# Routing logits as further columns of both products of stage one

## The chip, the cores and the metric

The kernel runs on one core of a Trainium2 chip. The metric is device time in microseconds for one execution; the median of three runs stands beside one profiled execution, whose trace is read below.

## The reference

```python
# x: (4, 512, 512) float32, ctx: (4 experts, 512, 512), 8 experts in the second layer
h = layernorm(x)                                  # (x - mean) / sqrt(var + 1e-5)
e1 = token_ids // 6250                            # expert of the first layer, by token id
a = h @ ctx[e1].T
x = x + (silu(a) * a) @ ctx[e1].T                 # the same ctx is gate, up and down matrix
h = layernorm(x)
idx = argmax(h @ router_w.T)                      # expert of the second layer, 8 logits
xq = act_quant(h)                                 # int8 steps by row
g, u = xq @ ternary(wg[idx]).T, xq @ ternary(wu[idx]).T
x = x + act_quant(relu(g) ** 2 * u) @ ternary(wd[idx]).T
```

`ternary(w)` rounds w / mean(|w|) to -1, 0 or 1 and scales back. There are 24 such matrices of 512 x 512.

## The kernel before

The 2048 rows are sorted by their first expert into B1 = 19 blocks of 128 rows (some padded), which stage one computes; stage two sorts them again by the chosen expert into B2 = 23 slots. Every engine has a queue that is written out by hand and runs in order; semaphores join them.

**Stage one** is a loop over ticks t. Both products of a block (`product1`, L1576) keep float32 accuracy with a high and a low half of each operand: hi x hi, hi x lo and lo x hi, each over K = 4 chunks of 128, so 12 matmuls of 512 columns in float32r. In tick t TensorE runs, in this order: transposes of p of block t-1 (L1560), first product of block t, `rank` of block t-3, transposes of the new row x1 of block t-2 (L1560, `transpose_x1`), transposes of h of block t+1, `sum_mean` (L1595), second product of block t-1, `logits` of block t-2 (L1668: x1 transposed, times router, 8 columns, float32, two instructions each), `count_in` of block t-3.

ScalarE in tick t: `evict_pT` (L739), `square` (L747), `silu` (L758), `evict_x1T` (L767, the copy of the transposed row that `logits` reads), `evict_hT` (L775), `scale_part` (L711, 1536 of the 2048 columns of a row of weight matrix t+2), in some ticks `scale_piece` (L731), `sum_abs` (L705) of weight matrix t+3, in some ticks `sum_piece` (L720).

VectorE in tick t: `residual` (L1121) of block t-2, `top_logits`, `choice` and `one_hot` of block t-3, `normalise`, `pT_rest` (L1110, the low half of p transposed), `largest`, `gate` (L1101), `mean_of` and `scale_of` (L1015, L1021) of matrix t+2, which release ScalarE's `scale_part`, its own `scale_part` (L1026, 512 columns), `row_index`, `hT_rest`, `moments_of`, and `cut` (L1032).

Two of the 24 weight matrices (21 and 22, `EXTRA`) don't fit the row of one a tick. Their sums are made in four pieces each, in ticks 3 to 6 and 11 to 14, and their scaling in three, in ticks 8 to 10 and 16 to 18.

SP issues the loads in order (`load_weights`, L382): matrix i waits until ScalarE and VectorE have scaled the matrix that had its buffer. The first extra matrix (L404) goes out behind weights 6, the second (L407) behind weights 14; behind weights 12 goes a 2 MB filler. After the last tick SP loads the rows of stage two (L411); loads 0 to 2 wait for matrix 20 to be scaled, loads 3 and 4 for matrix 21, by both engines:

```python
for s in range(EARLY):
    if s % 3 == 0:
        sp.wait_ge(dve_part, len(ORDER) - 1 + s // 3)
        sp.wait_ge(act_part, len(ORDER) - 1 + s // 3)
    load(s)
```

GpSimd gathers the rows of a block (L482), makes the scales of a row, and scatters it (L571) to the place of its expert.

Of the kernel before, what the change touches and what calls it, by code (L numbers as in the profile page):

```python
# [61 lines left out]

RING, ROWS = 5, 3
# [30 lines left out]
def moe_program(nc, x_in, tokens_in, ctx_in, router_in, weights_in, out):  # L94
    with ExitStack() as whole:
# [10 lines left out]
        bank = [whole.enter_context(nc.psum_tensor(f"bank{i}", [P, D], F32)) for i in range(8)]  # L106
# [10 lines left out]
        x1T = sb("x1T", [P, D], F32)  # L117
# [49 lines left out]
        best = sb("best", [P, 8], F32)  # L167
        best_at = sb("best_at", [P, 8], U32)
# [48 lines left out]
        with ExitStack() as inner:  # L217
            stack.append(inner)
            h = sb("h", [P, D], F32)
            hT_lo = sb("hT_lo", [P, D], F32R)  # L220
            ctx_hi = sb("ctx_hi", [P, E1 * K * D], F32R)
            ctx_lo = sb("ctx_lo", [P, E1 * K * D], F32R)
            stack.pop()
# [16 lines left out]
        assert ORDER[-1] % 3 == 2  # L240

# [28 lines left out]
        a_ps = [bank[4], bank[5]]  # L270
# [55 lines left out]
        x1T_ready, x1T_copied, logits_ready = (sem(n) for n in ("x1T_ready", "x1T_copied", "logits_ready"))  # L326
        best_ready, choice_ready, onehot_ready = sem("best_ready"), sem("choice_ready"), sem("onehot_ready")
# [39 lines left out]
        def _(sp):  # L367
# [5 lines left out]
            def load_weights(i):  # L373
# [58 lines left out]
        def _(pool):  # L432
# [53 lines left out]
            def high_halves(e):  # L486
# [3 lines left out]
                pool.tensor_copy(ctx_hi[:, e * K * D:(e + 1) * K * D], ctx_raw[e]).then_inc(pool_hi_ready, 1)  # L490
# [99 lines left out]
            for t in range(TICKS):  # L590
                if t >= 2:
                    gather(t + 3)
                if t < B1:
                    quantising(t - 2)
                    place(t - 3)
                    store(t - 3)
# [62 lines left out]
            place(B1 - 3)  # L659
            scale_of(B1 - 2)  # L660
            ratio_of(B1 - 2)
            store(B1 - 3)
            deviation_of(B1 - 1)
            place(B1 - 2)
            roots_of(B1 - 1)
            store(B1 - 2)
            scale_of(B1 - 1)
            place(B1 - 1)
# [15 lines left out]
        def _(act):  # L684
            act.preload_act_table(ACT.Silu)
            def high_halves(e):
                act.wait_ge(ctx_in_sem[e], 16)
                nc.scalar.activation(ctx_hi[:, e * K * D:(e + 1) * K * D], ctx_raw[e], ACT.Copy)\
                    .then_inc(ctx_hi_ready, 1)

            def sum_abs(i):
# [3 lines left out]
                if m == X_MATRIX:  # L695

                    act.wait_ge(x1_ready, X_USERS[-1] + 1)
                if m > EXTRA[1]:
# [25 lines left out]
            def scale_piece(x, j):  # L724
                m, first, end = EXTRA[x], EXTRA_CUTS[j], EXTRA_CUTS[j + 1]
                act.wait_ge(extra_scale_ready, x + 1)
                if j == 0:
# [23 lines left out]
            def silu(b):  # L751
# [4 lines left out]
                if b >= 1:  # L756
                    act.wait_ge(pT_ready, b)
                nc.scalar.activation(p[:, :], a_ps[b % 2][:, :], ACT.Silu, scale=rstd1[b % 2][:, :])\  # L758
                    .then_inc(sil_ready, 1)

            def evict_x1T(b):
                if not 0 <= b < B1:
# [4 lines left out]
                nc.scalar.activation(x1T[:, :], x1T_ps[:, :], ACT.Copy).then_inc(x1T_copied, 1)  # L767
# [86 lines left out]
            for t in range(2, TICKS):  # L854
# [4 lines left out]
                silu(t)  # L859
                evict_x1T(t - 2)  # L860
                evict_hT(t + 1)
                if t == 2:
# [12 lines left out]
            evict_x1T(B1 - 1)  # L875
# [30 lines left out]
        def _(dve):  # L906
# [94 lines left out]
            def low_half(e, part):  # L1001

                first = part * K * D // 2
                cols = slice(e * K * D + first, e * K * D + first + K * D // 2)
                if part == 0:
                    dve.wait_ge(*((ctx_hi_ready, e + 1) if e < 2 else (pool_hi_ready, e - 1)))
                ins = dve.tensor_tensor(ctx_lo[:, cols], ctx_raw[e][:, first:first + K * D // 2],  # L1007
                                        ctx_hi[:, cols].bitcast(F32), ALU.subtract)
                if part == 1:
                    ins.then_inc(ctx_lo_ready, 1)  # L1010

# [11 lines left out]
            def scale_part(i):  # L1023
                m = ORDER[i]
# [10 lines left out]
            def cut(i):  # L1035
                dve.wait_ge(dve_part, i + 1)
# [60 lines left out]
            def gate(b):  # L1097
# [3 lines left out]
                dve.scalar_tensor_tensor(p[:, :], a_ps[b % 2][:, :], rstd1[b % 2][:, :], p[:, :],  # L1101
# [11 lines left out]
            def residual(b):  # L1113
# [7 lines left out]
                dve.scalar_tensor_tensor(row[b % ROWS][:, 0:D], y_ps[:, :], 1.0, x[b % RING], ALU.mult,  # L1121
# [16 lines left out]

            def top_logits(b):
                if not 0 <= b < B1:  # L1140
                    return
                dve.wait_ge(logits_ready, b + 1)
                dve.max(best[:, :], logits_ps[:, 0:E2]).then_inc(best_ready, 1)

            def choice(b):
# [3 lines left out]
                dve.max_index(best_at[:, :], best[:, :], logits_ps[:, 0:E2]).then_inc(choice_ready, 1)  # L1149
# [258 lines left out]
            for t in range(2, TICKS):  # L1408
                interlude = early if t == EARLY_AFTER + 4 else iter(())
                residual(t - 2)  # L1410
                top_logits(t - 3)
                negative_mean(t - 2)
                next(interlude, None)
                choice(t - 3)
                next(interlude, None)
                one_hot(t - 3)
                next(interlude, None)
                normalise(t + 1)
                if t == 3:
# [3 lines left out]
                pT_rest(t - 1)  # L1423
                if t == 2:
# [6 lines left out]
                if t == 2:  # L1431
                    scale_part(3)
                next(interlude, None)
                gate(t)
# [489 lines left out]
```

## Time and profile before

| | us |
|---|---|
| median of 3 runs (lowest, highest) | 252.63 (252.18, 252.65) |
| the profiled execution | 252.44 |
| its span, first to last instruction | 250.5 |
| stage one, silu 0 to silu 18 | 21.66 to 162.75 |
| granted TensorE clock, mean | 0.993 |

"Busy" is the time in which an engine has an instruction running. Matmuls are pipelined, so the distance from one group's start to the next is what a group costs; its own duration is longer. "Idle before" is the engine's idle time ahead of an instruction, with what ended it.

### The profile page before, as it was taken

How to read it: one execution, taken by the hardware profiler on the slowest of the kernel's cores; microseconds unless marked ns; L12 is line 12 of the kernel's file. 1: busy time of each engine (PE TensorE's matmuls, PEld its weight loads, DVE VectorE, ACT ScalarE, POOL GpSimd, SP SyncE). 2: the span in 40 equal slices, each digit the busy share in tenths (PEclk: the TensorE clock that was granted, in tenths of full speed). 3: DMA queues.
4: the chain of work that ended last, by engine and by line, in shares of the span. 5: the costliest groups of instructions: out<-in, count | busy, mean ns of one | idle time of the engine just before them, and what ended most of it. 6: DMA issues, size and time to landing. Idle time of an engine off the chain costs nothing.

```text
span 250.5 us, 5540 instructions
## 1 busy us (share of the span) xinstructions
PE 230.1 (92%) x1319; PEld 168.0 (67%) x1327; DVE 216.7 (87%) x675; ACT 208.7 (83%) x324; POOL 166.1 (66%) x325
## 2 busy tenths in 40 slices
PE   2398999999999999999999999999989999999980
PEld 2245788888888888888888888887335445454430
DVE  5979999989898888898889888969999999999881
ACT  2767799799889888898889878888889999999970
POOL 4362675868778777778777745345737788686863
PEclk9999999999999999999999999999999999999997
DMA  5999953946753589885764545534358982212110
GB/s 194 425 357 361 429 210 107 377 154 238 252 184 102 193 306 404 285 311 207 252 218 139 176 185 213 174 98 152 99 149 258 303 294 93 99 69 79 66 42 0
DMA packets 13725, 51.70 MB, mean 206 GB/s; under 512 B 2750, under 2 KB 2750, under 8 KB 10112
## 3 DMA queue, kind: packets, MB, share of 16 engines
q1 hardware_dynamic: 8816, 37.91, 43.0%
q0 software_dynamic: 4880, 13.44, 14.6%
q8 instruction: 13, 0.21, 0.3%
q14 instruction: 16, 0.13, 0.1%
HBM read 40.49 MB, written 13.48 MB: 215 GB/s over the span
## 4 chain that ended last, share of the span: by engine, by line
PE 76%; DVE 11%; DMA 5%; ACT 3%; issue 3%; POOL 0%; SPq 0%; DVEq 0%; ACTq 0%
PE bank L1576 35%; PE bank L1698 22%; PE bank L1560 9%; PE bank L1668 5%; DMA ternary<-weight_chunks 3%; PE bank L1690 2%; PE bank L1802 2%; DVE ctx_lo L1007 1%; DMA staged<-x_rows 1%; PE bank L1595 1%; DVE ternary L964 1%; ACT ternary L705 1%; DVE p L1101 1%; DMA token_ids<-token_ids_in 1%; DVE ternary L1026 1%
## 5 line engine op out<-in xcount | busy, mean ns | idle before, releaser
L1698 PE MATMUL bank<-ternary,qT 128*128 x178 | 45.1, 379 | 0.5
L705 ACT ACTIVATE ternary<-staged 128x2048 bf16<-128x2048 f32 x20 | 38.0, 1900 | 2.0 <-DMA staged<-weight_chunks 2.0
L711 ACT ACTIVATE ternary<-staged,w_scale 128x1536 int16<-128x1536 f32 x20 | 31.4, 1576 | 2.3 <-DVE w_scale L1021 0.6
L571 POOL DMA_INDIRECT x_rows<-row,store_at x19 | 25.5, 1343 | 6.8 <-POOL store_at L563 5.0
L1698 PEld LDWEIGHTS bank<-ternary,qT 128*128 128x128 bf16 x184 | 17.2, 98 | 16.3 <-issue 1.0
L482 POOL DMA_INDIRECT x<-x_rows,gather x16 | 18.5, 1155 | 10.3 <-DVE gather L976 6.5
L652 POOL DMA_INDIRECT out_rows<-late_rows,late_token x18 | 19.6, 1089 | 7.9 <-DVE late_rows L1366 5.5
L1698 PE MATMUL bank<-ternary,rT 128*128 x90 | 23.4, 379 | 1.4 <-ACT rT L809 0.8
L758 ACT ACTIVATE p<-bank,rstd 128x512 f32<-128x512 f32 x19 | 13.0, 686 | 12.6 <-PE bank L1576 12.6
L1101 DVE SCALAR_TENSOR_TENSOR p<-bank,rstd,p 128x512 f32<-128x512 f32 x19 | 14.2, 749 | 9.6 <-ACT p L758 9.6
L1576 PE MATMUL bank<-ctx_hi,pT_hi 128*128 x76 | 22.3, 415 | 0.1
L1576 PE MATMUL bank<-ctx_hi,hT_hi 128*128 x76 | 22.4, 416 | 0.0
L1668 PEld LDWEIGHTS bank<-router,x1T 128*128 128x128 f32 x152 | 19.7, 191 | 2.0 <-ACT x1T L767 0.6
L1576 PE MATMUL bank<-ctx_lo,hT_hi 128*128 x76 | 20.4, 390 | 0.2 <-DVE ctx_lo L1007 0.2
L1576 PE MATMUL bank<-ctx_lo,pT_hi 128*128 x76 | 20.5, 392 | 0.0
L1576 PE MATMUL bank<-ctx_hi,pT_lo 128*128 x76 | 20.5, 392 | 0.0
L526 POOL TENSOR_TENSOR row<-ln,half_powers 128x2 f32<-128x2 f32 x19 | 14.5, 763 | 8.8 <-DVE squares L1136 8.7
L1576 PE MATMUL bank<-ctx_hi,hT_lo 128*128 x76 | 20.3, 389 | 0.0
L1668 PE MATMUL bank<-router,x1T 128*128 128x8 f32 x152 | 18.2, 246 | 0.1
L1312 DVE TENSOR_TENSOR prod<-bank,relu 128x512 f32<-128x512 f32 x23 | 15.9, 690 | 2.1 <-issue 0.8
L498 POOL TENSOR_TENSOR rstd<-var_eps,half_powers 128x1 f32<-128x1 f32 x19 | 13.7, 719 | 5.3 <-DVE var_eps L1077 4.8
L1576 PEld LDWEIGHTS bank<-ctx_lo,hT_hi 128*128 128x128 f32 x76 | 14.2, 188 | 3.6 <-issue 0.6
(237 smaller groups left out, 650.9 us busy)
## 6 DMA issues: line engine op xcount, KB each, us to landing
staged<-weight_chunks SPq DMA_DIRECT2D x20, 1024.0 KB, 5.4
late_rows<-x_rows SPq DMA_DIRECT2D x18, 260.0 KB, 3.7
ternary<-ctx_chunks SPq DMA_DIRECT2D x4, 1024.0 KB, 8.3
ternary<-weight_chunks SPq DMA_DIRECT2D x4, 1024.0 KB, 9.4
x_rows<-filler SPq DMA_DIRECT2D x1, 2080.0 KB, 12.6
staged<-x_rows SPq DMA_DIRECT2D x5, 260.0 KB, 2.9
x_rows<-row,store_at POOLq DMA_INDIRECT x19, 6.2
out_rows<-late_rows,late_token POOLq DMA_INDIRECT x18, 2.8
```

Of the source, the lines that this page charges most:

```text
L482: pool.indirect_dma_start(x[b % RING], None, x_in, bass.IndirectOffsetOnAxis(ap=gather1[:, b:b + 1], axis=0), bounds_check=last_token, oob ...
L526: pool.tensor_tensor(r[:, RSTD:INV + 1], s[:, 2:4], half_powers[:, :], ALU.pow).then_inc(norm2, 1)
L571: pool.indirect_dma_start(x1_rows, bass.IndirectOffsetOnAxis(ap=store_at[b % ROWS][:, :], axis=0), row[b % ROWS][:, :], None, bounds_check ...
L652: pool.indirect_dma_start(out, bass.IndirectOffsetOnAxis(ap=token, axis=0), cols_of([b], 0, D), None, bounds_check=last_token, oob_is_err= ...
L705: nc.scalar.activation(ternary[:, m * K * D:(m + 1) * K * D], staged_of(i), ACT.Abs, accum_out=abs_sum[:, 2 * i:2 * i + 1]).then_inc(abs_r ...
L711: nc.scalar.activation(ternary[:, m * K * D + DVE_COLS:(m + 1) * K * D].bitcast(I16), staged_of(i)[:, DVE_COLS:], ACT.Copy, scale=w_scale[ ...
L1101: dve.scalar_tensor_tensor(p[:, :], a_ps[b % 2][:, :], rstd1[b % 2][:, :], p[:, :], ALU.mult, ALU.mult).then_inc(p_ready, 1)
L1312: dve.tensor_tensor(prod[b % 2][:, :], u_ps[b % 2][:, :], relu2[:, :], ALU.mult)\
L1560: last = pe.transpose(ps[:, k * P:(k + 1) * P], src[:, k * P:(k + 1) * P], ident[:, :])
L1576: last = pe.matmul(ps[:, :], left[:, k * P:(k + 1) * P], right[:, bass.ds(e * (K * D) + k * D, D)], start=(n == 0 and k == 0), stop=(n == ...
L1668: last = pe.matmul(logits_ps[:, 0:E2], x1T[:, k * P:(k + 1) * P], router[:, k * E2:(k + 1) * E2], start=(k == 0), stop=(k == K - 1))
L1698: last = pe.matmul(ps[:, :], side(left[:, :], k), ternary[:, bass.ds(e * (3 * K * D) + (kind * K + k) * D, D)], start=(k == 0), stop=(k == ...
```

## The change

The logits of a block are (x + y) times router, where y is the second product. Since y = p x ctx^T, the part y x router is p times (ctx^T x router), and the part x x router is likewise 8 columns beside the first product (h instead of x: the same order of logits). So each context gets 8 further columns on either side: on the left the router, for the first product, on the right "contexts times router", for the second. From block FOLD = 5 on the logits are the sum of the two, and the x1 transposes, their copy and `logits` are left out.

- 520 columns don't fit one bank, so each matmul becomes two, of 256 and 264 columns, in halves of two neighbouring banks (`columns_of`). The first product has one buffer instead of two.
- Contexts times router is made once, in ticks 4 and 5 (`cr_products`: 32 matmuls for two experts, float32, 32 columns of stationary on each of four column groups), from four more transfers of 1 MB (the contexts by rows, `load_rows`), copied by ScalarE (`copy_cr`), transposed (`cr_transposes`) and split into halves by VectorE (`cr_halves`). GpSimd pads the router (`pad_router`).
- VectorE keeps the 8 logits of the first product (`keep_logits`, between gate and mean) and adds those of the second (`sum_logits`, ahead of the residual). The choice comes one tick earlier.
- From matrix SOLO = 9 on ScalarE scales all 2048 columns and VectorE none; SP's loads wait for ScalarE alone from there.
- The early slot tables are made in tick 17 instead of 18.

```diff
+FOLD = 5
+LEFT, RIGHT = E2, E2 + D
+WIDTH = D + 2 * E2
+CR_TICK = FOLD - 1
+SOLO = FOLD + 2 + 2
...
-                    sp.wait_ge(dve_part, last + 1)
+                    sp.wait_ge(dve_part, min(last + 1, SOLO))
                     sp.wait_ge(act_part, last + 1)
...
+            def load_rows(e):
+                sp.wait_ge(ctx_lo_ready, (0, 0, 1, E1 - 1)[e]) if e > 1 else None
+                sp.dma_start(ctx_rows[e], ctx_rows_in[e]).then_inc(ctx_rows_in_sem[e], 16)
+
             for i in range(4, len(ORDER)):
                 load_weights(i)
+                if i == 5:
+                    load_rows(0)
+                    load_rows(1)
+                if i == 6:
+                    load_rows(2)
+                    load_rows(3)
...
                 if s % 3 == 0:
-                    sp.wait_ge(dve_part, len(ORDER) - 1 + s // 3)
                     sp.wait_ge(act_part, len(ORDER) - 1 + s // 3)
...
             def scale_part(i):
-                m = ORDER[i]
+                m, first = ORDER[i], DVE_COLS if i < SOLO else 0
                 act.wait_ge(w_scale_ready, i + 1)
-                nc.scalar.activation(ternary[:, m * K * D + DVE_COLS:(m + 1) * K * D].bitcast(I16),
-                                     staged_of(i)[:, DVE_COLS:], ACT.Copy, scale=w_scale[:, m:m + 1])\
+                nc.scalar.activation(ternary[:, m * K * D + first:(m + 1) * K * D].bitcast(I16),
+                                     staged_of(i)[:, first:], ACT.Copy, scale=w_scale[:, m:m + 1])\
                     .then_inc(act_part, 1)
...
+            def keep_logits(b):
+
+                if not FOLD <= b < B1:
+                    return
+                dve.wait_ge(sil_ready, b + 1)
...
+                dve.tensor_copy(own_logits[b % 2][:, :], own_ps).then_inc(kept_ready, 1)
+
+            def sum_logits(b):
...
+                dve.wait_ge(y_ready, b + 1)
+                dve.wait_ge(kept_ready, b - FOLD + 1)
...
+                dve.tensor_tensor(summed[:, :], carried_ps, own_logits[b % 2][:, :], ALU.add).then_inc(summed_ready, 1)
...
-                interlude = early if t == EARLY_AFTER + 4 else iter(())
+                interlude = early if t == EARLY_AFTER + 3 else iter(())
...
                     for k in range(K):
-                        last = pe.matmul(ps[:, :], left[:, k * P:(k + 1) * P],
-                                         right[:, bass.ds(e * (K * D) + k * D, D)],
-                                         start=(n == 0 and k == 0), stop=(n == 2 and k == K - 1))
+                        for ps, first, columns in pieces:
+                            last = pe.matmul(ps, left[:, k * P:(k + 1) * P],
+                                             right[:, bass.ds(e * (K * WIDTH) + k * WIDTH + first, columns)],
+                                             start=(n == 0 and k == 0), stop=(n == 2 and k == K - 1))
...
+            def columns_of(b, second):
+
+                half = D // 2
+                if b < FOLD:
+                    return [(y_ps[:, :] if second else bank[4 + b % 2][:, :], LEFT, D)]
+                if second:
+                    return [(bank[2][:, half:], LEFT, half), (bank[3][:, 0:half + E2], LEFT + half, half + E2)]
+                return [(bank[4][:, half - E2:], 0, half + E2), (bank[5][:, 0:half], LEFT + half, half)]
+
+            def cr_products(pair):
...
+                for i in range(2):
+                    pe.wait_ge(ctx_rows_in_sem[2 * pair + i], 16)
+                    for k in range(K):
+                        for g in range(K):
+                            last = pe.matmul(cr_ps[g * 32:(g + 1) * 32, i * P:(i + 1) * P],
+                                             router_pad[:, k * 32:(k + 1) * 32],
+                                             ctx_rows[2 * pair + i][:, k * D + g * P:k * D + (g + 1) * P],
+                                             start=(k == 0), stop=(k == K - 1))
+                last.then_inc(cr_ready, 1)
...
             def transpose_x1(b):
-                if not 0 <= b < B1:
+                if not 0 <= b < FOLD:
                     return
...
             def logits(b):
-                if not 0 <= b < B1:
+                if not 0 <= b < FOLD:
                     return
...
+                if t == CR_TICK:
+                    cr_products(0)
+                if t in (CR_TICK + 1, CR_TICK + 2):
+                    cr_transposes(t - CR_TICK - 1)
...
                 sum_mean(t + ABOVE)
+                if t == CR_TICK + 1:
+                    cr_products(1)
                 second_product(t - 1)
...
             transpose_q(0)
             load_ffn_expert(0)
-            transpose_x1(B1 - 1)
             sum_mean(B1 + ABOVE)
+            rank(B1 - 1)
             gate_product(0)
-            logits(B1 - 1)
-            rank(B1 - 2)
```

## Rows read from the trace of the kernel before

**Rows 1.** The page's first part: busy time of each engine.
```profile
PE 230.1 (92%) x1319; PEld 168.0 (67%) x1327; DVE 216.7 (87%) x675; ACT 208.7 (83%) x324; POOL 166.1 (66%) x325
```

**Rows 2.** Windows, silu to silu: length, busy us (instructions) by engine, PEclk, DMA.
```profile
67.00:74.98 7.98, 7.98 (x50) 6.80 (x50) 7.30 (x25) 6.93 (x11) 6.03 (x11) 1.00 0.59 197
...
154.77:162.75 7.98, 7.98 (x50) 6.80 (x50) 6.83 (x31) 7.07 (x10) 3.24 (x7) 1.00 0.49 166
```

**Rows 3.** Timeline of TensorE over one tick: start us, duration us, what.
```profile
99.81 1.17 PE L1576 MATMUL bank<-ctx_hi,pT_hi 128*128 x4
...
102.64 0.95 PE L1668 MATMUL bank<-router,x1T 128*128 128x8 f32 x8
103.45 0.17 PE L1685 MATMUL bank<-onehot,from 128*128 128x8 bf16 x1
103.48 0.64 PE L1560 MATMUL bank<-ident,p 128*128 128x128 f32 x4
103.87 1.17 PE L1576 MATMUL bank<-ctx_hi,hT_hi 128*128 x4
104.88 1.07 PE L1576 MATMUL bank<-ctx_lo,hT_hi 128*128 x4
...
106.73 0.63 PE L1560 MATMUL bank<-ident,row 128*128 128x128 f32 x4
107.20 0.60 PE L1560 MATMUL bank<-ident,h 128*128 128x128 f32 x4
107.78 1.17 PE L1576 MATMUL bank<-ctx_hi,pT_hi 128*128 x4
```

**Rows 4.** Timeline of ScalarE, ticks with and without a piece.
```profile
74.98 0.69 ACT L758 ACTIVATE p<-bank,rstd 128x512 f32<-128x512 f32 x1 [0.95 <-PE bank L1576]
...
83.53 0.59 ACT L767 ACTIVATE x1T<-bank 128x512 f32<-128x512 f32 x1
...
84.72 1.58 ACT L711 ACTIVATE ternary<-staged,w_scale 128x1536 int16<-128x1536 f32 x1
86.20 0.87 ACT L731 ACTIVATE ternary<-ternary,w_scale 128x704 int16<-128x704 f32 x1
...
90.94 0.69 ACT L758 ACTIVATE p<-bank,rstd 128x512 f32<-128x512 f32 x1 [0.79 <-PE bank L1576]
...
146.80 0.69 ACT L758 ACTIVATE p<-bank,rstd 128x512 f32<-128x512 f32 x1 [1.44 <-PE bank L1576]
```

**Rows 5.** Timeline of all engines in one tick: from silu to the scaling.
```profile
106.90 0.68 ACT L758 ACTIVATE p<-bank,rstd 128x512 f32<-128x512 f32 x1
...
107.64 0.75 DVE L1101 SCALAR_TENSOR_TENSOR p<-bank,rstd,p 128x512 f32<-128x512 f32 x1
...
108.31 0.15 DVE L1015 TENSOR_SCALAR w_mean<-bank 128x1 f32<-128x1 f32 x1
...
108.69 0.49 DVE L1026 TENSOR_SCALAR ternary<-staged,w_scale 128x512 int16<-128x512 f32 x1
```

**Rows 6.** Timeline in tick 3: the extra matrix's issue, its first piece, the product behind.
```profile
43.04 0.33 SPq L404 DMA_DIRECT2D ternary<-weight_chunks  x1
...
49.91 0.63 ACT L720 ACTIVATE dump<-ternary 128x512 bf16<-128x512 f32 x1 [1.20 <-DMA ternary<-weight_chunks]
...
51.90 1.20 PE L1576 MATMUL bank<-ctx_hi,pT_hi 128*128 x4
```

**Rows 7.** A window of tick 3 (last two: DMA share, GB/s), and ScalarE in tick 10.
```profile
43.00:45.00 2.00, 2.00 (x14) 1.73 (x13) 2.00 (x6) 2.00 (x5) 0.87 (x3) 1.00 0.98 412
...
103.81 1.91 ACT L705 ACTIVATE ternary<-staged 128x2048 bf16<-128x2048 f32 x1 [0.79 <-DMA staged<-weight_chunks]
```

**Rows 8.** Timeline at the end of stage one: last scaling, and loads 3 and 4.
```profile
173.64 1.57 ACT L711 ACTIVATE ternary<-staged,w_scale 128x1536 int16<-128x1536 f32 x1
...
175.16 0.48 DVE L1026 TENSOR_SCALAR ternary<-staged,w_scale 128x512 int16<-128x512 f32 x1
...
176.77 1.46 SPq L411 DMA_DIRECT2D staged<-x_rows  x2
```

More of the change, by code:

```diff
@@ L104, in moe_program @@
         x1_rows = nc.dram_tensor("x1_rows", [SCRATCH_ROWS, ROW], F32).ap()
-        bank = [whole.enter_context(nc.psum_tensor(f"bank{i}", [P, D], F32)) for i in range(8)]
+        banks = whole.enter_context(nc.psum_tensor("banks", [P, 8 * D], F32))
+        bank = [banks[:, i * D:(i + 1) * D] for i in range(8)]
         ternary = sb("ternary", [P, MATS * K * D], BF16)
@@ L167, in moe_program @@
         best = sb("best", [P, 8], F32)
+        own_logits = [sb(f"own_logits{i}", [P, E2], F32) for i in range(2)]
+        summed = sb("summed", [P, E2], F32)
         best_at = sb("best_at", [P, 8], U32)
@@ L240, in moe_program, with whole_chunks, beside @@
         assert ORDER[-1] % 3 == 2
+        ctx_rows = [spare(m, 2 * K * D, F32) for m in (12, 14, 16, 20)]
+        early_home = spare(18, 2 * K * D // 2, F32)
+        x1T, router_pad = early_home[:, 0:D], early_home[:, D:D + P]
+        crT = early_home[:, D + P:D + 3 * P]
+        def whole_chunks(halves, e):
+            return halves[:, :].rearrange("p (e k w) -> p e k w", e=E1, k=K)[:, e, :, LEFT:RIGHT]
+        def beside(halves, first):
+            return halves[:, :].rearrange("p (e k w) -> p e k w", e=E1, k=K)[:, :, :, first:first + E2]
         staged_early = [spare(8, 2 * K * D, F32), spare(10, 2 * K * D, F32)]
@@ L592, in _ @@
                     gather(t + 3)
+                if t == 3:
+                    pad_router()
+                if t == FOLD + 3:
+                    place(FOLD)
+                    store(FOLD)
                 if t < B1:
                     quantising(t - 2)
-                    place(t - 3)
-                    store(t - 3)
+                    place(chosen(t)[0])
+                    store(chosen(t)[0])
                 if t >= 2:
@@ L726, in scale_piece @@
                 act.wait_ge(extra_scale_ready, x + 1)
+                if x == 0 and j == 0:
+                    act.wait_ge(crT_ready, E1 // 2)
                 if j == 0:
@@ L766, in evict_x1T, with copy_cr @@
                     act.wait_ge(logits_ready, b)
-                nc.scalar.activation(x1T[:, :], x1T_ps[:, :], ACT.Copy).then_inc(x1T_copied, 1)
+                else:
+                    act.wait_ge(ctx_lo_ready, 2)
+                nc.scalar.activation(x1T, x1T_ps[:, :], ACT.Copy).then_inc(x1T_copied, 1)
+            def copy_cr(pair):
+                act.wait_ge(cr_ready, pair + 1)
+                if pair >= 1:
+                    act.wait_ge(crT_ready, pair)
+                nc.scalar.activation(crT, cr_ps, ACT.Copy).then_inc(cr_copied, 1)
             def evict_hT(b):
@@ new lines, in cr_halves @@
+            def cr_halves(pair):
+                two = slice(2 * pair, 2 * pair + 2)
+                made_of = cr_ps.rearrange("p (e k w) -> p e k w", e=2, k=K)[:, :, :, 0:E2]
+                high, low = (beside(halves, RIGHT)[:, two] for halves in (ctx_hi, ctx_lo))
+                dve.wait_ge(crT_ready, pair + 1)
+                dve.tensor_copy(high, made_of).then_inc(cr_halves_ready, 1)
+                dve.wait_ge(cr_halves_ready, 2 * pair + 1)
+                dve.tensor_tensor(low, made_of, high.bitcast(F32), ALU.subtract).then_inc(cr_halves_ready, 1)
@@ L1137, in largest, with logits_of @@
                                   accum_out=ln2[b % 2][:, 3:4]).then_inc(largest_ready, 1)
+            def logits_of(b):
+                return logits_ps[:, 0:E2] if b < FOLD else summed[:, :]
             def top_logits(b):
@@ L1408, in _ @@
             for t in range(2, TICKS):
-                interlude = early if t == EARLY_AFTER + 4 else iter(())
+                interlude = early if t == EARLY_AFTER + 3 else iter(())
+                first, *second = chosen(t)
+                sum_logits(t - 2)
                 residual(t - 2)
-                top_logits(t - 3)
+                if t == FOLD + 3:
+                    row_index(FOLD)
+                top_logits(first)
                 negative_mean(t - 2)
                 next(interlude, None)
-                choice(t - 3)
+                choice(first)
                 next(interlude, None)
-                one_hot(t - 3)
+                one_hot(first)
                 next(interlude, None)
+                for b in second:
+                    top_logits(b)
                 normalise(t + 1)
+                for b in second:
+                    choice(b)
+                    one_hot(b)
                 if t == 3:
@@ L1444, in _ @@
                 if t < B1:
-                    row_index(t - 3)
+                    row_index(first)
                 next(interlude, None)
@@ L1561, in transpose1, with product1 @@
                 return last
-            def product1(ps, hi, lo, e, b=None, ahead=None):
+            def product1(pieces, hi, lo, e, b=None, ahead=None):
                 pairs = [(hi, ctx_hi), (hi, ctx_lo), (lo, ctx_hi)]
@@ L1661, in logits @@
             def logits(b):
-                if not 0 <= b < B1:
+                if not 0 <= b < FOLD:
                     return
```

172 lines of the change are left out of this document (120 added, 52 removed).

## The prediction

> **What bounds the kernel now.** I read the page first: TensorE is busy for 92% of the span and its next rival, VectorE, for 87% [rows 1]. An average over two stages says little, so I cut stage one at each silu with the windows view. From silu 7 (74.98 us) to silu 18 (162.75) are eleven ticks of 7.98 us, and TensorE is busy for all of such a tick, while VectorE and ScalarE are busy for about 7 [rows 2, 4]. The reader is to see that TensorE sets the tick, and that what comes next is only one microsecond below. The timeline of TensorE then splits a tick, from one second product to the next (99.81 to 107.78, 7.97 us): second product 2.83; logits 0.81; transposes of p 0.39; first product with the rank behind it 2.86; transposes of the new row 0.47; transposes of h 0.44; the rest is a mean and a count [rows 3]. The change takes 0.81 + 0.47 = 1.28 us out of it, if nothing else comes to bind.
>
> What else can bind is read from ScalarE's queue, which is strictly in order: silu, x1T copy, hT copy, scaling of a weight matrix, a piece of an extra matrix in some ticks, absolute sum of the next matrix, pT copy, square, and the next silu. Its idle time before the next silu is its whole slack: 0.79 us in a tick with a scaling piece, 0.95 with a summing piece, 1.44 with none [rows 4]. What starts the scaling is not the x1T copy in front of it but VectorE: gate 0.74 us after the silu, mean and reciprocal after it; the scaling starts 1.79 us after the silu [rows 4, 5].
>
> **The change part by part.**
>
> 1. *Products in halves.* Each 512-column matmul becomes one of 256 and one of 264 columns, each with its own weight load: 24 pairs in place of 12. No row shows a 4-byte matmul of 256 columns with its load. Twelve of 512 take 2.83 us; its first four take 0.10 more than the next four (1.17 against 1.07 [rows 3]), so one costs 0.228 beside 0.09 once, of which 512 columns at 2.4 GHz are 0.213. Take 256 columns (0.107) away: 0.121, and 0.125 for 264; a product is 12 x 0.246 + 0.09 = 3.04, or 0.21 more. From below, the loads bound it: eight loads with 8-column matmuls come every 0.10 to 0.11, four transposes of 128 columns too [rows 3], so 24 x 0.11 = 2.6, a gain of 0.2. From above, load and stream not overlapped, 0.11 + 0.11 each: 5.3. The 512-column stream overlaps its loads and so do the transposes, so I take 3.04. TensorE's tick: 7.97 - 1.28 + 0.42 = 7.11 us.
>
> 2. *ScalarE.* The x1T copy (0.59) goes, but the scaling waits for VectorE anyway, so its place becomes idle time and gives nothing. From matrix 9 (tick 7) ScalarE scales all 2048 columns. From 704 to 1536 columns it grows by 0.71 us [rows 4], 0.85 ns a column, so 512 more cost 0.44. Keeping the 8 logits on VectorE stands between gate and mean and so ahead of the scaling: about 0.10, between nothing and the 0.15 that the small instruction there takes [rows 5]. ScalarE's cycle grows by 0.54: 7.98 - 0.79 + 0.54 = 7.73 in a tick with a scaling piece, 7.98 - 0.95 + 0.54 = 7.57 with a summing piece, 7.98 - 1.44 + 0.54 = 7.08 with none. That is above TensorE's 7.11 in all ticks but those without a piece: ScalarE becomes the bound and takes back more than half of the gain.
>
> 3. *VectorE.* It loses 0.4 (its part of the scaling [rows 5]) and gains two instructions of 8 columns: 7.30 in tick 6 to 7 [rows 2] becomes about 7.2. It hides behind the others except in tick 7 (7.2). In tick 17 it now makes the early slot tables as well, formerly a tick later: 31 instructions against 25 [rows 2] show the kind of load; I charge 0.3 there.
>
> 4. *Ticks 7 to 17.* 7.2 + 3 x 7.73 + 4 x 7.57 + 7.11 + 7.73 + 8.0 = 83.5 us, against 11 x 7.98 = 87.8: a gain of 4.3. (Scaling pieces are in ticks 8 to 10 and 16 to 18, summing pieces in 3 to 6 and 11 to 14.)
>
> 5. *Ticks 5 and 6* still do old work for blocks 3 and 4, and have four split products, 4 x 0.21, and four transposes of contexts times router, 4 x 0.11: +1.3.
>
> 6. *Contexts times router.* Per pair of experts 32 float32 matmuls of 128 columns, each two instructions; a 4-byte transpose of 128 columns takes 0.11 [rows 3], so 64 x 0.11 = 7.0 us if nothing overlaps, 1.8 if the four column groups run together. No row shows column groups. 64 loads and 64 matmuls must also be issued, so I take 3.5. The second pair stands in tick 5 ahead of the second product, with TensorE full: +3.5 (1.8 to 7.0). The Trainium skill, "TensorE: Matmul & The Clock Gate", section Part 3, measured 2.38 times for three column tiles. By that the pair would take 2.9 and the sum would be 0.6 lower, an estimate; no row here shows it. The first pair stands in tick 4 and is hidden, as follows.
>
> 7. *The new transfers.* Four matrices of 1 MB. The first two go out behind weights 5, when the engines are full, but nothing waits for what is behind them. The other two are issued on SP behind weights 6, ahead of the first extra matrix, which goes out at 43.04. ScalarE already waits 1.20 us for that matrix in tick 3 and starts its piece at 49.91; pT copy, square, silu are queued behind, VectorE's pT_lo behind those, and TensorE's second product starts at 51.90 because of it [rows 6]. At 412 GB/s, with the engines 98% busy in that stretch [rows 7], 2.1 MB more are 5.1 us. So ScalarE, then VectorE, then TensorE stand 5.1 us later: +5.1. The first pair of step 6 runs in this hole, as it stands on TensorE before the blocked product; at 7.0 it would stick out by 1.9.
>
> 8. *A later collision.* In tick 10 ScalarE waits 0.79 us for weights held up by the 2 MB of filler and an extra matrix [rows 7]; before, its slack took that. Now it has none, and the tick before is a quarter of a microsecond shorter: +1.1 (0 to 1.5).
>
> 9. *End of stage one.* The last silu's block takes as long as before: the pT copy of block 18 waits for scaling and piece on ScalarE, and the work taken out of TensorE there filled that wait. What improves is what follows: loads 3 and 4 of stage two go out at 176.77, after VectorE's part of the last scaling (175.16 + 0.48), itself behind ScalarE's start at 173.64 [rows 8]. Without VectorE's part the release is ScalarE's end, some 0.5 earlier, and choice and store of block 18 come earlier too. I take -0.7; the bounds are 0 and -2.5 (three logits and transposes that stood there, 0.81 + 0.47 each, less what waits hid).
>
> Sum: +5.1 +3.5 +1.3 -4.3 +1.1 -0.7 = +6.0. The profiled execution took 252.44 us (span 250.5), 0.2 below the median of 252.63, so I go from it: 258.4 us.
>
> **The rivals.**
>
> *A. Column groups don't overlap.* 7.0 a pair: +3.5 in tick 5 and +1.9 in tick 4: 263.8. For it: no row shows a group running beside another. Against: separate columns and separate outputs.
>
> *B. Faster: ScalarE doesn't take over.* Place: the stretch from silu to silu in ticks 7 to 17. If the full scaling and the kept logits fit into the slack, TensorE and VectorE set some 6.9 us: 11 x 6.9 = 75.9, 7.6 less than step 4, and the collision of step 8 is absorbed: 249.7. It decides when the mean tick falls below about 7.05, as 6.0 + 4.3 = 10.3 us have to come from 11 ticks. For it: 0.59 of ScalarE's work goes. Against: the mean's arrival at 1.79, not the copy, starts the scaling.
>
> *C. The transfer doesn't hold the extra matrix up*, because the rows are landed beside it. The 5.1 go, the first pair of step 6 loses its cover, +3.5: 256.8. Against: engines at 98%.
>
> *D. Weight loads are not hidden in halves of this length.* Each pair costs 0.22; a product 5.3 + 0.09 against 2.83; TensorE's tick 11.8. 11 x 3.8 = 42 lost instead of 4.3 won, 10 more in ticks 5 and 6, 5 at the end: about 320. Against: transposes and loads of [rows 3]. The Trainium skill, "TensorE: Matmul & The Clock Gate", section Part 3, says that weight loads overlap matmuls in flight only when the row groups differ, which is this rival. The trace does not agree: 512-column matmuls with full-height loads come every 0.23 us and not every 0.32.
>
> **How the numbers follow.** Chances: forecast with its terms 0.42 (its own range 255 to 261), A 0.13, B 0.24, C 0.16, D 0.03, no change at all 0.02. The range leaves out D and the far part of B, and takes A with both bounds: 250.3 to 264.0. Within 0.2% of the median (about what a measurement of this kernel can tell) is 252.1 to 253.1; B with a late tail or C with cheap column groups could land there, 0.05. Faster 0.25, slower 0.70.
>
> **What would show it.** Right: TensorE idle for some microseconds near 52 to 57 us, before a second product, with ScalarE waiting about 6 us for the extra matrix; silu to silu near 7.7 and 7.6 in ticks 8 to 14; no idle time of ScalarE before silu, some 0.7 before its scaling, and TensorE idle half a microsecond a tick; a product at 3.0. Wrong: silu to silu at 7.1 or below in ticks with pieces (B); ScalarE's wait for the extra matrix still at 1.2 (C); a pair of contexts times router near 7 (A) or a product above 3.4 (D).

## The result, and the profile after

| | before | after |
|---|---|---|
| median, us | 252.49 (4 runs, 252.18 to 252.65) | 260.66 (4 runs, 259.46 to 263.36) |
| ratio, 95% interval | | 1.031 (1.027 to 1.035) |
| profiled execution / its span | 252.44 / 250.5 | 259.46 / 257.4 |
| silu 0 to silu 18 | 21.66 to 162.75 | 21.41 to 169.19 |
| granted TensorE clock, mean | 0.993 | 0.979 |

The change makes the kernel 3.1% slower; 258.4 was forecast, in a range of 250.3 to 264.0. The execution of 263.36 us is a slow one and not in the ratio; the median of the other three is 260.37. The profiled execution is the fastest of the four, so where its parts are added up below they make 7.0 us (6.9 of span), not the 8.2 between the medians.

The page's first part, kernel after:

```profile
PE 225.7 (88%) x1619; PEld 176.6 (69%) x1627; DVE 214.6 (83%) x696; ACT 206.9 (80%) x312; POOL 162.9 (63%) x327
```

Against [rows 1] every engine but the weight loads is busy for less time, and the kernel takes longer: the work did go down, and what grew is waiting. A gain counted in busy time would have been read here where there is none. Where the time went is seen by laying silu against silu, before and after:

| stretch | before | after | difference |
|---|---|---|---|
| up to silu 4 | 51.73 | 57.48 | +5.75 |
| silu 4 to 5 | 7.28 | 9.02 | +1.74 |
| silu 5 to 7 | 15.97 | 19.39 | +3.42 |
| silu 7 to 18 | 87.77 | 83.30 | -4.47 |
| silu 18 to the end of the span | 87.75 | 88.21 | +0.46 |

**Up to silu 5.** Timeline of ScalarE and then of TensorE, kernel after, in ticks 3 to 5 (start us, duration us, what, idle before and what ended it):

```profile
55.66 0.63 ACT L785 ACTIVATE dump<-ternary 128x512 bf16<-128x512 f32 x1 [6.47 <-DMA ternary<-weight_chunks]
```

```profile
50.76 1.96 PE L1733 MATMUL banks<-ternary 128*32 128x128 f32 x64
52.65 0.18 PE L1857 MATMUL banks<-onehot,before 128*128 128x8 bf16 x1
...
53.59 0.28 PE L1761 MATMUL banks<-abs_sum,ones 128*128 128x1 f32 x2
57.65 1.19 PE L1708 MATMUL banks<-ctx_hi,pT_hi 128*128 x4 [3.77 <-DVE pT_lo L1228]
58.68 1.67 PE L1708 MATMUL banks<-ctx_lo,pT_hi 128*128 x4
60.15 1.91 PE L1708 MATMUL banks<-ctx_hi,pT_lo 128*128 x4
61.85 1.20 PE L1847 MATMUL banks<-router,ternary 128*128 128x8 f32 x8
...
63.32 1.21 PE L1708 MATMUL banks<-ctx_hi,hT_hi 128*128 x8
64.37 1.13 PE L1708 MATMUL banks<-ctx_lo,hT_hi 128*128 x8
65.34 1.12 PE L1708 MATMUL banks<-ctx_hi,hT_lo 128*128 x8
66.30 0.38 PE L1744 MATMUL banks<-ident,ternary 128*128 128x128 f32 x2
...
67.66 1.95 PE L1733 MATMUL banks<-ternary 128*32 128x128 f32 x64
69.54 1.19 PE L1708 MATMUL banks<-ctx_hi,pT_hi 128*128 x4
```

ScalarE's wait for the extra matrix, 1.20 us in [rows 6], is 6.47; the blocked second product starts at 57.65 instead of 51.90. SP issues the extra matrix at 43.06, where the kernel before issued it at 43.04 [rows 6], so it is the transfer that takes longer, not its issue that comes later. The first pair of contexts times router (50.76 to 52.65) lies ahead of the hole (the idle time of 3.77 us on TensorE) and costs nothing. Behind the hole the first group still takes 1.03, as elsewhere, but the next two, which take 0.91 to 0.94 elsewhere, take 1.47 and 1.70: the clock has fallen. It was granted at 1.00 all through the hole, fell at 59.0, 1.3 us after TensorE had started again, and was back at 1.00 at 62.4. A window of that place (busy us by engine, then granted clock, DMA share, GB/s):

```profile
59.00:60.00 1.00, 1.00 (x4) 0.81 (x3) 0.93 (x6) 1.00 (x2) 0.90 (x3) 0.50 0.00 0
```

0.50 is the lower level, 1.2 GHz; in the kernel before the clock was 1.00 in every such window of stage one. The rest is read off the same timeline: a product in halves takes 2.98 us (63.32 to 66.30), a pair of contexts times router 1.88 (67.66 to 69.54).

**Silu 7 to 18.** Timeline of ScalarE, kernel after, a tick with a scaling piece (the answer to [rows 4]):

```profile
92.93 0.69 ACT L825 ACTIVATE p<-banks,rstd 128x512 f32<-128x512 f32 x1
93.52 0.59 ACT L849 ACTIVATE hT_hi<-banks 128x512 fp32r<-128x512 f32 x1
94.90 2.00 ACT L776 ACTIVATE ternary<-staged,w_scale 128x2048 int16<-128x2048 f32 x1 [0.79 <-DVE w_scale L1136]
96.81 0.87 ACT L798 ACTIVATE ternary<-ternary,w_scale 128x704 int16<-128x704 f32 x1
...
100.66 0.67 ACT L825 ACTIVATE p<-banks,rstd 128x512 f32<-128x512 f32 x1
```

```profile
113.93 1.91 ACT L770 ACTIVATE ternary<-staged 128x2048 bf16<-128x2048 f32 x1 [1.08 <-DMA staged<-weight_chunks]
```

The silus of ticks 7 to 18 lie at 85.89, 92.93, 100.66, 108.25, 117.02, 124.47, 131.94, 139.40, 146.86, 153.70, 161.32 and 169.19. The reader is to see that silu has lost its idle time in front (0.79 to 1.44 in [rows 4]): ScalarE goes straight from its square to the next silu, and its one gap, 0.79 here and 0.70 in most ticks, lies ahead of the scaling, where the x1T copy was. ScalarE sets the tick, 7.73 here. Windows of a tick with a summing piece and of one with none (the answer to [rows 2]):

```profile
124.47:131.94 7.47, 7.17 (x60) 6.99 (x60) 6.31 (x24) 6.77 (x13) 5.47 (x11) 1.00 0.66 216
146.86:153.70 6.84, 6.59 (x56) 6.50 (x57) 6.35 (x25) 6.13 (x10) 4.45 (x10) 1.00 0.57 199
```

TensorE is no longer busy throughout, and ScalarE and VectorE are busy for less still; that ScalarE sets the tick is seen from its queue, not from these shares. The tick of 8.77 (108.25 to 117.02) is the later collision: the second fence above, 1.08 us of waiting for weights where 0.79 were harmless in [rows 7]. That the filler is what holds these weights up was not tried by a run.

**End of stage one.** Timeline of TensorE, kernel after:

```profile
174.42 1.21 PE L1708 MATMUL banks<-ctx_hi,pT_hi 128*128 x8 [1.35 <-ACT pT_hi L806]
...
179.84 0.18 PE L1857 MATMUL banks<-onehot,before 128*128 128x8 bf16 x1 [0.71 <-DVE onehot L1281]
180.26 0.81 PE L1877 MATMUL banks<-ternary,qT 128*128 x3 [0.24 <-issue]
```

The first product of stage two starts 11.1 us after silu 18 (180.26 - 169.19), where it was 10.3. It stands behind `rank` of block 18 on TensorE, and that waits for VectorE's choice of the same block. A window right behind it shows the half clock a second time; in the kernel before the clock was 1.00 there too:

```profile
182.00:184.00 2.00, 2.00 (x7) 0.76 (x6) 1.59 (x4) 1.23 (x4) 1.59 (x3) 0.50 0.21 30
```

### The profile page after: what moved, and what is told of

Its sections match the earlier page's. It is cut to its first block, busy times and chain, and to the rows that moved or that the text cites. A ratio compares the mean times of both kernels' runs of the same rounds, so it can differ in the third digit from the quotient of the medians.

```text
span 257.4 us, 6374 instructions
## 1 busy us (share of the span) xinstructions
PE 225.7 (88%) x1619; PEld 176.6 (69%) x1627; DVE 214.6 (83%) x696; ACT 206.9 (80%) x312; POOL 162.9 (63%) x327
## 4 chain that ended last, share of the span: by engine, by line
PE 39%; DVE 20%; DMA 15%; issue 14%; ACT 9%; POOL 2%; DVEq 0%; ACTq 0%; POOLq 0%; SPq 0%
PE banks L1877 19%; PE banks L1708 11%; DMA staged<-weight_chunks 9%; DMA ternary<-weight_chunks 5%; DVE pT_lo L1228 3%; DVE squares L1254 2%; ACT ternary L776 2%; DVE p L1219 2%; PE banks L1869 2%; ACT ternary L770 2%; PE banks L1691 2%; ACT pT_hi L806 2%; PE banks L1981 2%; POOL out_rows L715 1%; DVE row L1239 1%
## 5 line engine op out<-in xcount | busy, mean ns | idle before, releaser
L1877 PE MATMUL banks<-ternary,qT 128*128 x179 | 46.6, 389 | 0.6 <-issue 0.2
L776 ACT ACTIVATE ternary<-staged,w_scale 128x2048 int16<-128x2048 f32 (+1 forms) x20 | 37.0, 1854 | 10.4 <-DVE w_scale L1136 10.4
L1708 PE MATMUL banks<-ctx_hi,pT_hi 128*128 x132 | 22.9, 313 | 9.5 <-DVE pT_lo L1228 7.7
L1708 PEld LDWEIGHTS banks<-ctx_hi,pT_hi 128*128 128x128 f32 x132 | 17.6, 188 | 11.1 <-issue 6.8
L1877 PE MATMUL banks<-ternary,rT 128*128 x89 | 23.0, 380 | 1.3 <-ACT rT L883 0.8
L1708 PE MATMUL banks<-ctx_hi,hT_hi 128*128 x132 | 22.8, 312 | 0.0
L1708 PE MATMUL banks<-ctx_hi,pT_lo 128*128 x132 | 22.1, 307 | 0.0
L1708 PE MATMUL banks<-ctx_lo,pT_hi 128*128 x132 | 21.8, 305 | 0.0
L1708 PE MATMUL banks<-ctx_lo,hT_hi 128*128 x132 | 21.4, 301 | 0.2 <-DVE ctx_lo L1083 0.2
L1708 PE MATMUL banks<-ctx_hi,hT_lo 128*128 x132 | 21.1, 299 | 0.0
L1708 PEld LDWEIGHTS banks<-ctx_hi,pT_lo 128*128 128x128 f32 x132 | 18.8, 193 | 1.1
```

Of the source, the lines that this page charges most:

```text
L776: nc.scalar.activation(ternary[:, m * K * D + first:(m + 1) * K * D].bitcast(I16), staged_of(i)[:, first:], ACT.Copy, scale=w_scale[:, m:m ...
L1708: last = pe.matmul(ps, left[:, k * P:(k + 1) * P], right[:, bass.ds(e * (K * WIDTH) + k * WIDTH + first, columns)], start=(n == 0 and k == ...
L1877: last = pe.matmul(ps[:, :], side(left[:, :], k), ternary[:, bass.ds(e * (3 * K * D) + (kind * K + k) * D, D)], start=(k == 0), stop=(k == ...
```

## The experiments

**1. Rows behind weights 7.** Is the stall the order of the transfers?

```diff
-                if i == 6:
+                if i == 7:
                     load_rows(2)
                     load_rows(3)
```

> The changed kernel, but the last two 1 MB matrices of contexts by rows go out behind weights 7 instead of weights 6, so that they stand behind the extra matrix. Theory (the transfers stand in front of the extra matrix, and the stall behind it also lets TensorE's clock fall): ScalarE's wait for the extra matrix falls from 6.5 to about 1.2 us, the second product of tick 3 to 4 starts near 52 instead of 57.65, TensorE shows no stretch at half clock there; 7 us less, 253 to 254. Rival (the 2 MB cost the same wherever they stand, since the DMA engines are the bound there): the wait turns up at the sum of matrix 7 or 8 or at contexts times router, and the time stays at 257 or above.

253.65 us, ratio to before 1.001 (0.997 to 1.004): the whole loss is gone by moving two transfers, as the theory had it. ScalarE and TensorE in this run:

```profile
50.17 0.63 ACT L785 ACTIVATE dump<-ternary 128x512 bf16<-128x512 f32 x1 [0.66 <-DMA ternary<-weight_chunks]
```

```profile
51.07 1.95 PE L1733 MATMUL banks<-ternary 128*32 128x128 f32 x64
...
54.05 1.17 PE L1708 MATMUL banks<-ctx_hi,pT_hi 128*128 x4
55.06 1.10 PE L1708 MATMUL banks<-ctx_lo,pT_hi 128*128 x4
```

The wait is 0.66, there is no hole, and no stretch at 0.50 follows. What the hole had covered now shows: the first pair stands ahead of the second product with nothing idle, and silu 4 to 5 takes 9.34. From silu 4 to 7 this run takes 28.73 us against 23.25 before: 5.5 us, of which 3.8 are the two pairs; the shorter ticks 7 to 17 (83.6 against 87.8) give most of it back. The later collision stands elsewhere here: ticks 10 and 12 take 7.83 and 8.70.

**2. The transfers alone.** The kernel before, with `load_rows` at the places of the change; nothing reads what they bring. The only other edit makes ScalarE's first writes over the four buffers, some ticks later, wait until the transfers have landed.

```diff
+                if i == 5:
+                    load_rows(0)
+                    load_rows(1)
+                if i == 6:
+                    load_rows(2)
+                    load_rows(3)
```

> The kernel before, with nothing of the change but its four transfers of 1 MB at their places in SP's queue (nothing reads them; the first writes over them wait until they have landed). Theory (the transfers alone make the stall): ScalarE waits about 6.5 us for the extra matrix, and the time is 5 to 7 us above before, 258 to 259. Rival (the stall needs the changed work of tick 3 and 4 as well): at most 1 us above before.

259.32 us, ratio 1.024 (1.020 to 1.028), just above the 258 to 259 expected. ScalarE waits 6.98 us for the extra matrix, silu 4 comes at 56.73, and TensorE:

```profile
56.90 2.08 PE L1594 MATMUL bank<-ctx_hi,pT_hi 128*128 x4 [5.88 <-DVE pT_lo L1128]
58.78 1.63 PE L1594 MATMUL bank<-ctx_lo,pT_hi 128*128 x4
60.25 1.09 PE L1594 MATMUL bank<-ctx_hi,pT_lo 128*128 x4
```

Here the hole is 5.88 long, as no contexts times router lie ahead of it, and the first group behind it takes nearly twice its time (1.88 from start to start, 1.01 elsewhere). This time the clock falls inside the hole, at 53.2, and is back at 60.0. So the transfers make the stall by themselves, and the clock's fall with it.

**3. Halves alone.** The kernel before, each matmul of the products as two of 256 columns in the same bank.

```diff
-                        last = pe.matmul(ps[:, :], left[:, k * P:(k + 1) * P],
-                                         right[:, bass.ds(e * (K * D) + k * D, D)],
...
+                        for c in range(2):
+                            last = pe.matmul(ps[:, c * half:(c + 1) * half], left[:, k * P:(k + 1) * P],
+                                             right[:, bass.ds(e * (K * D) + k * D + c * half, half)],
...
```

> The kernel before, with each 512-column matmul of both products of stage one as two of 256 columns in the same bank, each with its own weight load; nothing else. Theory (a pair of halves costs little more than the whole, 2.95 to 3.0 us a product against 2.83): 38 products, up to 0.16 us each with TensorE the bound, so 4 to 6 us slower, 257 to 258.5. Rival (weight loads are not hidden behind 256 columns): 5.3 us a product, over 330.

255.56 us, ratio 1.008 (1.005 to 1.012). TensorE in this run:

```profile
101.53 1.21 PE L1578 MATMUL bank<-ctx_hi,pT_hi 128*128 x8
102.57 1.12 PE L1578 MATMUL bank<-ctx_lo,pT_hi 128*128 x8
103.53 1.12 PE L1578 MATMUL bank<-ctx_hi,pT_lo 128*128 x8
104.49 0.95 PE L1671 MATMUL bank<-router,x1T 128*128 128x8 f32 x8
```

A product takes 2.96 (101.53 to 104.49) against 2.83, and a tick 8.22 against 7.98: 0.12 us a product. Rival D is excluded. The whole comes out 1.4 us below what I expected (257 at least). In the profiled execution the 13 ticks from silu 5 to 18 are 3.2 us longer (106.90 against 103.74); before silu 5 the dearer products cost only 0.5.

**4. VectorE keeps its part of the scaling.** The changed kernel with SOLO out of reach, and its last part and SP's wait for it put back.

```diff
-SOLO = FOLD + 2 + 2
+SOLO = 99
```

> The changed kernel, but VectorE keeps its 512 columns of every scaling, as before. Theory (ScalarE's queue from silu to silu sets the ticks from 7 on): ScalarE's cycle is 0.43 us shorter, but VectorE's is 0.4 longer, at about 7.3 to 7.4; the ticks with a scaling piece fall from 7.7 to 7.4, those with a summing piece from 7.46 to 7.3 or 7.4, those without a piece rise from 6.9 to 7.3; 1 us less in all, 259 to 260. Rival (TensorE or the transfers set the ticks): no tick changes by over 0.1 us.

257.71 us, ratio 1.018 (1.014 to 1.022), about 3 us below the changed kernel's and below the 259 to 260 that I expected. Ticks 7 to 17 take 80.8 us (85.69 to 166.50) instead of 83.3. Windows of this run, a scaling piece and a summing piece:

```profile
92.73:100.40 7.67, 7.30 (x62) 7.11 (x61) 7.56 (x29) 6.62 (x10) 6.38 (x12) 1.00 0.73 239
123.08:130.49 7.41, 7.36 (x62) 7.27 (x63) 7.07 (x25) 6.45 (x13) 6.00 (x12) 1.00 0.63 217
```

Three of the four ticks with a summing piece are 7.03 or 7.04, where the changed kernel has 7.46: all of the 0.43 comes back, and VectorE with its share of the scaling still does such a tick in 7.0. Two ticks gain little: tick 8 (the first window), where VectorE has a second matrix to cut and is busy for 7.56, and tick 12 (the second), in which ScalarE waits 0.89 for VectorE's scale and starts its scaling 2.23 us behind the silu instead of 1.86. So ScalarE set the ticks, and moving the 512 columns to it took 2.5 us of a possible gain of 7.0; I had expected VectorE to stop the tick at 7.3.

**5. Clock held by added matmuls.** The changed kernel, 14 matmuls of constants ahead of the blocked product, and 13 in the idle time of TensorE at the end of stage one.

```diff
...
+                if t == CR_TICK:
+                    pe.wait_ge(x1_ready, CR_TICK - 1)
+                    warm_up(14)
                 second_product(t - 1)
...
+            warm_up(4, 0)
             second_product(B1 - 1)
+            warm_up(1, 0)
             rank(B1 - 2)
...
+            warm_up(3, 1)
             sum_mean(B1 + ABOVE)
+            warm_up(4, 1)
             rank(B1 - 1)
+            warm_up(1, 1)
             gate_product(0)
```

> The changed kernel with matmuls of constants added on TensorE, whose results are overwritten: 14 in tick 4 ahead of the blocked second product, and 13 in small groups in the idle time at the end of stage one. Theory (in both places TensorE's idle time, which the change made, is followed by a stretch at half clock that costs time): the stretch at clock 0.50 behind 58 us goes, silu 5 comes 1.5 to 1.7 us earlier; the one behind 182 us goes too, and the end comes another 1 to 2 us earlier: 257 to 258 against 260.4. Rival (the clock falls where TensorE has slack and costs nothing): silu 5 and the end stay within 0.3 us, or come later by the added matmuls.

258.75 us, ratio 1.024 (1.021 to 1.028); 257 to 258 was expected. TensorE in this run, behind the hole, and a window at the end of stage one:

```profile
54.28 3.18 PE L1981 MATMUL banks<-iota 128*128 128x512 f16 x14
58.29 1.19 PE L1708 MATMUL banks<-ctx_hi,pT_hi 128*128 x4 [0.82 <-DVE pT_lo L1228]
59.32 1.09 PE L1708 MATMUL banks<-ctx_lo,pT_hi 128*128 x4
60.24 1.09 PE L1708 MATMUL banks<-ctx_hi,pT_lo 128*128 x4
```

```profile
182.00:184.00 2.00, 1.95 (x10) 0.85 (x10) 1.59 (x5) 1.61 (x4) 1.61 (x4) 1.00 0.03 8
```

The stall is as long (a wait of 6.56 us), but silu 4 to 5 takes 7.45 instead of 9.02: 1.57 us were the clock's. At the end of stage one the half clock is gone too, and silu 18 to the end takes 88.1 instead of 88.2: there it cost nothing that shows. That the chain of VectorE and ScalarE sets the time there would explain it (in the trace of the changed kernel above, TensorE's waits of 1.35 and 0.71 are for them), but this was not shown apart. The theory holds for the first place and falls for the second.

**6. Edits 1 and 4 together.**

> The changed kernel with the rows behind weights 7 and with VectorE's 512 columns of every scaling (both single edits together). If the two causes are independent, their gains add: 253.7 less 2.5 to 3.3 is 250.4 to 251.2, and ticks of 7.4 with a scaling piece, 7.0 without. Rival (with the early stall gone, the transfers collide with the shorter ticks): 252.5 or more, with ScalarE waiting over 1 us for weights in two ticks.

251.51 us, ratio 0.995 (0.993 to 0.997): the routing as further columns is faster than the kernel before, by half a per cent, once its transfers and its scaling stand elsewhere. The sum of the two gains, 250.4 to 251.2, is missed by 0.3. Silu 18 is at 161.91 against 162.75 before. The rival has a part in the miss: ScalarE waits 1.41 us for weights in tick 10, so ticks 7 to 17 take 81.3 and not 80.8.

**7. The same, logits kept later, and TensorE filled at the end.**

> As the run with both edits, and the 8 logits are kept after the mean and its reciprocal instead of ahead of them, and 13 matmuls of constants fill TensorE's idle time at the end of stage one. Theory: 0.1 us in each of the five ticks with a scaling piece, and 1 to 2 us at the end if the clock is held there: 249 to 250. Rival (the clock's fall there costs nothing, or the added matmuls stand in the way): the same as the run with both edits, or 0.5 us more.

251.26 us, ratio 0.994 (0.992 to 0.997), not told apart from the run before it; the 249 to 250 expected did not come. Ticks 7 to 17 take 80.9 instead of 81.3. Silu 18 to the end of the span is 87.6 in both, with the clock at 0.50 near 174 us in run 6 and at 1.00 here: held or fallen, the clock at the end of stage one makes no difference.

**8. Logits kept after the mean.** A single execution.

```diff
-                keep_logits(t)
                 if t < B1:
                     mean_of(t + ABOVE)
...
                     scale_of(t + ABOVE)
+                    keep_logits(t)
```

> The changed kernel, but VectorE keeps the 8 logits after mean and reciprocal. Theory (ScalarE's scaling is started by the reciprocal, and ScalarE sets the ticks with a piece): the scaling starts 0.08 us earlier behind its silu, and each tick of 8 to 14, 16 and 17 is 0.08 us shorter, 0.7 us in all. Rival (the scaling waits for the hT copy, or ScalarE does not set the ticks): no change.

Of the four ticks with a summing piece three take 7.37 to 7.39, where the changed kernel has 7.45 to 7.47; the first of them, right behind the collision, takes 8.35, with the clock at 0.50 from 122 to 124 us. So 0.08 us a tick, as expected; the ticks with a scaling piece scatter more (8, 9, 16 and 17 differ by -0.19, +0.08, -0.09 and -0.06). The whole, 261.44, says nothing: in this run the collision of tick 10 was a wait of 2.93 us instead of 1.08, and the stretch at half clock at the first hole lasted nearly twice as long (0.50 from 57 to 63), and silu 4 to 5 took 9.92 instead of 9.02.

**9. One column group after the other.** A single execution: do the four groups run together, or is a narrow stationary cheap?

```diff
-                    for k in range(K):
-                        for g in range(K):
+                    for g in range(K):
+                        for k in range(K):
```

> The changed kernel with the two inner loops of contexts times router exchanged: the four chunks of one column group follow each other, and then the next group; the same 64 instructions on 32 columns. Theory (the 1.9 us of a pair come from four column groups running at the same time): matmuls of the same group can't overlap, so the pair takes 64 x 0.11 = 7.0 us, and silu 6 comes about 5 us later than in the changed kernel. Rival (each instruction costs 0.03 us because its stationary has only 32 columns): the pair still takes 1.9.

TensorE in this run:

```profile
66.40 4.33 PE L1733 MATMUL banks<-ternary 128*32 128x128 f32 x64
70.65 1.20 PE L1708 MATMUL banks<-ctx_hi,pT_hi 128*128 x4
```

4.25 us a pair, between the theory's 7.0 and the rival's 1.9: 0.066 an instruction against 0.029 with the groups in turn. Groups in turn save a factor of 2.26, which fits groups that run beside each other. It isn't the only reading: in sequence, neighbouring matmuls also add into the same output, and no run separates the two. And the same group in sequence costs less than the 0.11 of a transpose of 128 columns, which I had taken as the price without overlap; the runs don't show what makes up the 0.066. The Trainium skill, "TensorE: Matmul & The Clock Gate", section Part 3, has 2.38 times for three column tiles of 512 columns. The trace has about the same, 2.26, with four tiles of 128 columns.

This run bears on the clock as well. The longer first pair fills more of the hole, TensorE is idle for only 1.05 us in front of the blocked product (57.95), the clock stays at 1.00, and silu 4 to 5 takes 7.45, as in run 5. So the 1.6 us come back without any added matmul.

## Why the prediction was right

| step | forecast | measured |
|---|---|---|
| 1 product in halves | +0.21 | +0.15 (after), +0.13 (run 3) |
| 2 ticks 8 to 10 | 7.73 each, +1.1 in tick 10 | 7.73, 7.59, 8.77 |
| 2 ticks 11 to 14 | 7.57 | 7.45 to 7.47 |
| 3 tick 7 | 7.2 | 7.04 |
| 4, 8 silu 7 to 18, with the ticks above | -4.3 + 1.1 = -3.2 | -4.47 |
| 5, 6 silu 5 to 7 | +1.3 + 3.5 = +4.8 | +3.42 |
| 7 up to silu 4 | +5.1 | +5.75 |
| clock behind the hole | not in the sum | +1.74 (1.57 by run 5) |
| 9 end of stage one | -0.7 | +0.46 |
| sum of the span | +6.0 | +6.9 |

*Step 7 was the deciding one and held*: the two transfers stand ahead of the extra matrix, and its wait blocks three engines in turn. Shown by run 2 (the transfers alone cost 2.4%) and run 1 (moving them takes away the loss). It came out 0.65 larger than 2.1 MB at 412 GB/s; what makes up the 0.65 stays open.

*What the sum lacked was the clock.* The step "the first pair of step 6 runs in this hole" saw the idle time and stopped there. The hole still left TensorE idle for 3.77 us, and a stretch at half clock followed, which cost 1.6 (runs 5 and 9).

*Steps 2 and 4 held in their mechanism.* ScalarE's scaling starts 1.86 us after its silu in most ticks (100.66 to 102.52; 1.97 in tick 8) and takes 2.00, against 1.89 and 2.01; the tick is ScalarE's. Run 4 shows it from the other side. The ticks with a piece are within 0.14 of the forecast, tick 10 with its 1.1 among them, and the two with none are 0.16 and 0.27 shorter (7.04 against 7.2, 6.84 against 7.11). All but tick 8 err to the same side, and over eleven ticks that is 1.3 us. One error was VectorE: by step 3 it needs 7.2 without the scaling, so I thought it would be the next bound at 7.3 to 7.4 with it. It needs about 7.0.

*Step 6, the size.* 3.5 for a pair was the middle of 1.8 and 7.0; it is 1.88, near the lower end. Too high by 1.6, which happens to cover the clock: luck, not insight.

*Step 9, the sign.* That second product 18 would start at the same distance from its silu holds (5.23 against 5.13). What I placed behind it did not: the new order puts `rank` of block 18 ahead of the first gate product, so that the choice of block 18, formerly off the path, holds up stage two (0.71 us of waiting in the trace). That this order is the whole cause of the 0.46 wasn't tried, and the 0.46 is itself no firm number: runs 1, 8 and 9 have the same end of stage one and take 87.97, 87.33 and 87.97 there, against 87.75 before. What they do show is that no 0.7 is won in any of them.

*The sum.* The total of +6.9 lies 0.9 from the +6.0, but the parts are off by +0.65 (step 7), +1.74 (the clock), -1.38 (steps 5 and 6), -1.27 (steps 4 and 8) and +1.16 (step 9). The direction and the deciding step were right for the stated reason; that the total came this near is in good part luck.

*Rivals.* A is excluded by the trace (1.88 a pair), B by the ticks (mean 7.57, not below 7.05), C by run 2, D by run 3. The medians differ by 1.2 us more than the profiled executions; 0.3 of it is the slow execution, and the rest stays open. The wait of tick 10 was 1.08 us in one execution of the changed kernel and 2.93 in one of its near copy (run 8), and silu 4 to 5 took 9.02 and 9.92 in the same two, so this collision and the length of the stretch at half clock are where I would look.

## What to carry to other kernels

- A transfer has a place in a queue, and what it costs is the wait of whatever stands behind it. Ask for each new load which load it is put ahead of, and who is already waiting for that one. Here two lines in the order of SP were worth 2.7%, more than the whole edit to the compute.
- When the engine that sets the tick is relieved by one microsecond and the next one is one microsecond below, the gain is that of the tightest queue afterwards. Moving work onto an engine because something was taken off it pays only if the work removed was on its path; here the place of the removed copy became a wait for VectorE's scale.
- Idle time of TensorE has a second price, the clock behind it, where TensorE is what the rest waits for; where it isn't (end of stage one), that price is nothing.

## What the runs showed of the hardware

- Float32 matmuls of 128 columns on 32 columns of stationary: 0.029 us an instruction with four column groups in turn (1.88 / 64), 0.066 in the same group (4.25 / 64, run 9).
- A 256-column half costs 0.123 us with its own weight load (2.96 / 24, run 3): cutting each matmul of a product of twelve in two, so that the same weights are loaded twice, adds 0.12 to 0.15 us to the product.
- After 3.77 us of idle TensorE in stage one of the changed kernel the clock ran on at 1.00 for 1.3 us of new work and was then at 0.50 for 3.4 us. In run 2, with 5.88 us idle, it fell inside the idle time. After 0.82 us (run 5) and 1.05 us (run 9) it stayed at 1.00.
